# A macaron block on one core: the router's logit difference on VectorE, the three-part split of B without casts, and nine steps of the slot table moved by one or two slots

## The reference, cut to what matters

```python
x = x + 0.5 * ffn(layernorm(x))        # f = 0
x = x + mamba(layernorm(x))
x = x + 0.5 * ffn(layernorm(x))        # f = 1

def ffn(x):                            # 8 experts of width 176, top 2; shared part of width 352
    logits, idx = top_k(x @ Wg, 2)
    w = one_hot(idx) weighted with softmax(logits)
    y = sum_e w[:, e] * ((silu(x @ W1[e]) * (x @ W2[e])) @ W3[e])
    return y + (silu(x @ Ws1) * (x @ Ws2)) @ Ws3

def mamba(x):                          # inner width 256, 16 states
    x_in, z = split(x @ W_in + b_in)
    xc = silu(conv4(x_in)); B, C = split(xc @ W_xp + b_xp); delta = softplus(xc @ W_dt + b_dt)
    h = exp(delta * A) * h + delta * xc * B         # scan over 256 tokens, for each of 16 states
    y = (sum over states of h * C + D * xc) * silu(z)
    return alpha * normalised(x + y @ W_out + b_out) + beta
```

## Time and profile before

| | |
|---|---|
| median of 3 runs | 1952.55 us (1949.0 to 1955.74) |
| the profiled execution | 1954.8 us, its span 1953.0 us |
| PE busy | 1685.0 us, 86% |
| DVE busy | 1528.1 us, 78% |
| POOL busy | 1435.9 us, 74% |
| ACT busy | 1216.9 us, 62% |
| mean granted TensorE clock | 0.950 of full speed |

### The profile page before, as it was taken

One profiled execution on the slowest core, in us unless ns is written; L12 is line 12 of the kernel. 1 busy time (PEld: TensorE's weight loads), 2 busy tenths in 40 slices (PEclk: granted clock), 3 DMA queues, 4 the chain that ended last, 5 costly groups with the idle time before them and its releaser, 6 DMA issues.

```text
span 1953.0 us, 27826 instructions
## 1 busy us (share of the span) xinstructions
PE 1685.0 (86%) x7378; PEld 1006.3 (52%) x7378; DVE 1528.1 (78%) x2337; ACT 1216.9 (62%) x1828; POOL 1435.9 (74%) x1350
## 2 busy tenths in 40 slices
PE   2896868999989899899989899898989999967488
PEld 1553535555545555555545555555555555544255
DVE  2237988988878888788878898888889898888732
ACT  1265657676856767586766767676676767665322
POOL 2336767788878778688877878788877878887853
PEclk9897969999989999999999999999999999988698
DMA  4124756776766857577665767667585867767742
GB/s 133 38 82 117 186 119 175 166 184 164 177 159 152 192 146 190 142 169 183 166 167 145 186 166 174 170 158 189 147 197 138 204 165 173 180 149 176 160 102 65
DMA packets 121342, 305.10 MB, mean 156 GB/s; under 512 B 19299, under 2 KB 40518, under 8 KB 106822
## 3 DMA queue, kind: packets, MB, share of 16 engines
q0 software_dynamic: 18432, 125.84, 31.9%
q1 hardware_dynamic: 94976, 173.07, 30.7%
q10 hardware_dynamic: 7750, 4.10, 0.8%
HBM read 167.67 MB, written 5.24 MB: 89 GB/s over the span
## 4 chain that ended last, share of the span: by engine, by line
PE 37%; issue 18%; POOL 14%; DVE 13%; DMA 11%; ACT 5%; ACTq 1%; DVEq 1%; POOLq 0%; SPq 0%
PE ps_y L1062 9%; DVE hist L903 6%; POOL prod L579 5%; POOL gated L517 5%; DMA yacc<-prod 5%; PE ps_h1b L1048 5%; PE ps_h2b L1070 5%; PE ps_h1a L1048 4%; PE ps_h2a L1070 4%; PE ps_m L1019 3%; DMA wrow<-w_rows 3%; PE ps_m L1113 3%; DMA out<-xres 2%; PE ps_m L1009 2%; DVE gated L883 1%
## 5 line engine op out<-in xcount | busy, mean ns | idle before, releaser
L579 POOL TENSOR_TENSOR prod<-hist,crow 128x1024 f32<-128x1024 f32 x224 | 566.6, 2530 | 239.6 <-DVE hist L903 237.7
L1062 PEld LDWEIGHTS ps_y<-down_w,gated 128*128 128x128 f32 (+1 forms) x3584 | 474.3, 196 | 267.4 <-issue 165.0
L903 DVE TENSOR_TENSOR_SCAN hist<-decay,ps_db 128x1024 f32<-128x1024 f32 x256 | 583.6, 2280 | 2.9
L517 POOL TENSOR_TENSOR gated<-gated,silu 128x512 f32<-128x512 f32 x352 | 484.6, 1440 | 93.9 <-DVE gated L883 81.2
L1062 PE MATMUL ps_y<-down_w,gated 128*128 128x128 f32 (+1 forms) x3584 | 489.5, 281 | 40.8 <-DVE xres L890 22.7
L855 DVE TENSOR_TENSOR ps_db<-du,ps_db 128x1024 f32<-128x1024 f32 x256 | 313.1, 1223 | 185.4 <-PE ps_db L1030 183.0
L667 ACT ACTIVATE decay<-delta,a_neg 128x510 f32<-128x510 f32 x512 | 327.0, 709 | 3.6 <-DVE hist L903 2.2
L687 ACT ACTIVATE silu<-ps_h1a 128x512 f32<-128x512 f32 (+1 forms) x224 | 133.0, 594 | 223.5 <-PE ps_h1a L1048 223.3
L1070 PE MATMUL ps_h2a<-xnT,up_w 128*128 128x512 f32 (+1 forms) x448 | 236.2, 609 | 22.9 <-DVE gated L883 22.7
L1048 PE MATMUL ps_h1b<-xnT,up_w 128*128 128x512 f32 x448 | 240.7, 619 | 3.5 <-ACT silu L687 3.5
L1070 PE MATMUL ps_h2b<-xnT,up_w 128*128 128x512 f32 x448 | 231.5, 599 | 8.5 <-DVE gated L883 8.5
(11 more groups left out here) (139 smaller groups left out, 1915.3 us busy)
## 6 DMA issues: line engine op xcount, KB each, us to landing
yacc<-prod POOLq DMA_DIRECT2D x112, 1024.0 KB, 9.4
crow<-c_rows SPq DMA_DIRECT2D x128, 512.0 KB, 4.6
wrow<-w_rows SPq DMA_DIRECT2D x320, 128.0 KB, 5.0
wrow<-w_rows SPq DMA_DIRECT2D x64, 224.0 KB, 7.2
wrow<-w_rows SPq DMA_DIRECT2D x64, 192.0 KB, 6.2
...
```

Of the source, the lines that this page charges most:

```text
L517: nc.gpsimd.tensor_tensor(gated[:, pos % NGATE, :], gated[:, pos % NGATE, :], silu[:, (pos + NCHUNK * f_parity(of, f)) % NSILU, :], ALU.mu ...
L579: nc.gpsimd.tensor_tensor(prod[:, (pair - 1 + odd) % 2, s % 2, :, :], hist[:, s % 2, :, :], c_all, ALU.mult).then_inc(prod_done, 1)
L903: nc.vector.tensor_tensor_scan(hist[:, s % 2, :, :].rearrange("p h t -> p (h t)"), decay[:, s % NA, :, :, :].rearrange("p h b t -> p (h b ...
L1062: ins = nc.tensor.matmul(ps_y[:, t * C:(t + 1) * C], gated[0:rd, posd % NGATE, t * P:(t + 1) * P], down_w[0:rd, jd, :], start=(posd == 0 a ...
```

## The change

1. `drop0` and `drop1` leave POOL. DVE makes the difference inside `route`, where a one-element memset stood between the maxima and the indices.
2. `bparts` is done without casts: the first part comes straight from PSUM plus bias with a bf16 output, the others are subtractions with bf16 outputs. Six instructions and four waits become five and a memset, with three waits.
3. Table: `addy0` one slot earlier (4 to 3); `route0` one later (10 to 11), `tilt0` one earlier (13 to 12); `stats1` and `scale1` one earlier (to 19 and 20); `route1`, `tilt1`, `weights1` one earlier (to 25, 27, 28); `delta` two later (24 to 26).
4. The last chunk of the second layer moves from slot 16 to 17, and with it the work that follows it by one, two and four slots.
5. SP issues the rows of C (`c6`) ahead of the weights' rows `w0:3`.

```diff
-        0: ["stats0"], 1: ["scale0"], 2: ["norm0"], 3: ["fold"], 4: ["addy0", "xT0"], 5: ["stats2", "scale2", "logits0"],
+        0: ["stats0"], 1: ["scale0"], 2: ["norm0"], 3: ["addy0", "fold"], 4: ["xT0"], 5: ["stats2", "scale2", "logits0"],
...
-    UNIT = {s: (1, pos) for pos, s in enumerate((0, 1, 2, 3, 4, 5, 6, 7, 8, 10, 12, 14, 15, 16))}
+    UNIT = {s: (1, pos) for pos, s in enumerate((0, 1, 2, 3, 4, 5, 6, 7, 8, 10, 12, 14, 15, 17))}
...
-                        elif step == "drop0" and enters(k) or step == "drop1" and tail(k):
-                            pool.wait_ge(top_ready, route_no(k, step) + 1)
-                            nc.gpsimd.tensor_tensor(drop[:], top[:, :, 0], top[:, :, 1], ALU.subtract
-                                                    ).then_inc(drop_ready, 1)
...
                             dve.wait_ge(top_ready, route_no(k, step) + 1)
-                            nc.vector.memset(carrier[:], 0.0)
+                            nc.vector.tensor_tensor(drop[:], top[:, :, 0], top[:, :, 1], ALU.subtract
+                                                    ).then_inc(drop_ready, 1)
...
-                            nc.vector.tensor_tensor(
-                                bc[:], ps_m[:, 0:TILES * 2 * NS].rearrange("p (t n) -> p t n", t=TILES),
-                                b_xp_b[:].unsqueeze(1).to_broadcast([P, TILES, 2 * NS]), ALU.add
-                            ).then_inc(misc_taken, 1)
-                            dve.wait_ge(misc_taken, turn(k, "xproj"))
-                            chain = Chain(dve, dve_bc, 4, k + 1)
-                            split(chain, bc[:, :, 0:NS], brem[:], brem2[:], bparts, NS).then_inc(bparts_ready, 1)
+                            chain = Chain(dve, dve_bc, 3, k + 1)
+                            rows_in = ps_m[:, 0:TILES * 2 * NS].rearrange("p (t n) -> p t n", t=TILES)
+                            bias = b_xp_b[:].unsqueeze(1).to_broadcast([P, TILES, 2 * NS])
+                            hi, md, lo = (bparts[:, :, 32 * q:32 * q + NS] for q in range(PARTS))
+                            nc.vector.tensor_tensor(bc[:], rows_in, bias, ALU.add)
+                            chain.link(nc.vector.tensor_tensor(hi, rows_in[:, :, 0:NS], bias[:, :, 0:NS], ALU.add))
+                            nc.vector.tensor_tensor(brem[:], bc[:, :, 0:NS], hi, ALU.subtract).then_inc(misc_taken, 1)
+                            chain.link(nc.vector.tensor_tensor(md, bc[:, :, 0:NS], hi, ALU.subtract))
+                            chain.link(nc.vector.tensor_tensor(lo, brem[:], md, ALU.subtract))
+                            nc.vector.memset(carrier[:], 0.0).then_inc(bparts_ready, 1)
```

More of the change, by code:

```diff
@@ L837, in stats_no @@
                 return before(k, stats_list) + stats_list(k).index(which)
-            def split(chain, whole, rem, rem2, parts, width):
-                hi, md, lo = (parts[:, :, 32 * q:32 * q + width] for q in range(PARTS))
-                chain.link(nc.vector.tensor_copy(hi, whole))
-                chain.link(nc.vector.tensor_tensor(rem, whole, hi, ALU.subtract))
-                chain.link(nc.vector.tensor_copy(md, rem))
-                chain.link(nc.vector.tensor_tensor(rem2, rem, md, ALU.subtract))
-                return nc.vector.tensor_copy(lo, rem2)
             def input_term(g, par, s):
```

1 line of the change is left out of this document (removed), and 12 rows, old and new, of tables (PLAN, SP_PLAN).

## The result

Before: 1954.14 us, median of 4 runs (1949.0 to 1957.9). Changed: 1922.26 us, median of 4 runs (1919.37 to 1923.06). The ratio is 0.9836, interval 0.981 to 0.9862: faster by 31.9 us, 1.6%. The profiled execution took 1919.37 us with a span of 1917.5; PE is busy 1670.5 us (87%), DVE 1546.6 (81%), POOL 1433.3 (75%), ACT 1222.6 (64%).

What follows compares the result with a forecast made beforehand. PE was taken as the bound, through its idle waits. The terms summed to 4.3 us per body, rounded to 4.0, times 12 is 48, plus 7 outside: 1954.8 - 55 = 1900, or 1898 at the median; range 1880 to 1918.

Steps and rivals of the forecast that it cites:

- the rival at 1935: New waits, at `dt1` for ACT and at `row_b` for state 14, take most of the gain; 1935 us, chance 0.18.
- `addy0`, +1.7: `addy0` one slot sooner: PE's wait of 1.74 us for `xres` goes, gaining 1.7 us per body.
- `resid`, +0.3: `resid` ahead of the routing: PE's 0.65 us wait for `rtok` goes, half counted, +0.3 us per body.
- The last chunk, -0.7: Last chunk in slot 17: the 0.81 us wait for `bounce` is covered, a 1.5 wait for `dpre` comes; -0.7 per body.
- `stats1`, 0: `stats1` one slot sooner moves into DVE's wait of 2.43 us in slot 19; no gain or loss.
- The split, +0.3: Split without casts: the wait for POOL moves to the subtraction, two small instructions behind it are saved; +0.3 us per body.
- `route1` ahead of the scan, -0.7: Routing with `drop` on DVE before scan 13: the scan comes 2.3 us later, PE's `row_b` waits 1.4; -0.7 per body.
- `weights1`, +2.4: `weights1` one slot sooner, no `drop` on POOL: PE's whole 2.49 us wait for `wtok` goes; +2.4 per body.
- The clock, +0.8: Slow PE matmuls behind the wait for `wtok` go in six of twelve bodies; +0.8 us per body on average.
- The rest, +0.2: Rows of weights that DVE waits for in slot 26 of some bodies, now later in its order; +0.2 us per body.
- The four bodies outside, 7 us: The four bodies outside the loop, with the same waits, were to give some 7 us.
- The slower rival: DVE's routing waits twice for POOL, at `drop` and at `hot`, delaying every scan behind; 1976 us, chance 0.09.

Runs made afterwards that it cites:

- The early release: Changed kernel with the PSUM tile given back by a memset right behind its two reads instead of by `brem`; 1916.96 us, ratio 0.9797.
- The routing put back: Changed kernel with `route1`, `tilt1`, `weights1` and `delta` in their old slots, `drop` still on DVE; 1934.7 us, ratio 0.9895.
- the second run: The changed kernel measured again, unedited, on the chip of the other kernels of its call; 1920.86 us, ratio 0.9823.
- the parts measured alone: Kernel before with only `addy0` in slot 3 (1935.88 us), only the new split (1949.29), or only the last chunk, `stats1`, `scale1` and `c6` moved (1960.57).
- the first group: First of three groups of kernel runs, each beside the kernel before on its own chip; there eleven counted runs of before spread from 1941.75 to 1967.34 us.

## Why the prediction was right, and where its numbers were not

The direction held, and the mechanism in the main: PE's waits went, and DVE's slack at the end of the body paid for them (2.80 to 4.46 before, 1.3 to 2.2 after). The forecast was 56 us and 31.9 came; 1922 lies above the forecast's own range (1880 to 1918), inside that of 8 in 10, and nearer to the rival at 1935 than to 1898. The body was to be 107 us and is 108.5. By its own steps:

- **`addy0`, +1.7: right.** Alone it shortens the loop by 14.6 us, and the time by 13 to 34, where 12 times 1.7 is 20.
- **`resid`, +0.3: not measured alone.** The waits of PE for `rtok`, 7.8 us over the twelve bodies, are gone.
- **The last chunk, -0.7, and `stats1`, 0: about right together.** The wait for `dpre` was to be 1.5 and is 0.52. I had not seen that POOL's `gated`, one slot later with its chunk, would be late by 0.70. 0.8 gained less 1.2 lost is -0.4; the measurement says 0 with 0.5 per body either way (6 us over twelve). In the changed kernel the transpose waits 0.36 for `zs` too, which the step had as a bound, and 0.8 less 1.6 is close to the -0.7. `stats1` waits 2.26 for POOL's `xres` (835.11), about the 2.43 that DVE waited there before.
- **The split, +0.3: right in what happens, too small to be measured.** `brem` takes 2.16 at the median, the write of the first part 0.21. The Trainium skill ("SBUF — State Buffer", Who interferes with whom) says that a DVE instruction with two inputs in SBUF contends with a GpSimd instruction that reads SBUF, and the trace agrees for 0.21 against 2.16. What I missed is that `brem` also gives the PSUM tile back, so that PE waits 1.40 for it. The early release shows that this wait costs nearly nothing, since other waits for DVE take its place.
- **`route1` ahead of the scan, -0.7: right at DVE, not on POOL.** `drop` takes 1.35 against the 1.4 expected, `hot` 0.69 against 0.5. (The items of the sum, 0.35, 1.4, 0.9 and 0.5, give 3.15 and not 3.4.) PE's wait for the scan is 0.41 in every second body against 1.4. The step that failed is that I followed the later scan to `row_b` alone. POOL's product of state 13 waits for that scan as well (2.86 us in each body, where before it was 0 to 2.2), and a `gated` that PE needs stands behind it.
- **`weights1`, +2.4, "The whole wait goes": this is where the forecast missed.** The wait for `wtok` did go, as said. But PE meets 2.34 for POOL's `gated` in the slot before, because of the later product. The routing put back exchanges one for the other (29.9 us of waits for `wtok` against 27.9 for `gated`), and moving that one `gated` ahead of the product gives about 15 us more (1922.26 and 1920.86 against 1906.37). That is most of the 24 us that were missing.
- **The clock, +0.8: half of it, and for the same reason.** What the clock lacks falls from 0.17 to 0.12 of a body, which is 0.05 times 110 us or 0.5 per body (0.3 by the second run, with 0.14). Behind the new wait PE's clock still falls in six bodies of twelve. In body 7 the four groups behind it take from 976.39 to 981.01, 4.62 us, where body 6 takes 2.94 for the same four (869.09 to 872.03): 1.7 lost in such a body, 0.8 on average over twelve, which I had booked as won. With the `gated` earlier the clock is at 1.00 (the level of 2.4 GHz) in all twelve bodies, and PE is busy 100.8 per body instead of 101.4. The step also priced a fall of the clock at 1.7 wherever it stands. Ahead of the back edge it cost more, as told below.
- **The rest, +0.2: right in direction.** DVE's waits for rows of weights fall from 8.6 us in seven bodies to 0.3 in one.
- **The four bodies outside, 7 us:** the span outside the loop was 617.8 and is 615.2, so 2.6 came.
- **The slower rival** (routing that waits twice for POOL) did not form: `drop` at most 2.15 and `hot` at most 0.71, never both long. The rival in which new waits take most of the gain came nearest in kind, with 1935; it named ACT and `row_b`, and the wait stood on POOL. The sign of being wrong, `tilt0` held for more than 1 us right behind `drop`, did not show: it waits 0.5.

What no step of the sum had is the back edge of the loop. DVE at the end of body 7 before, PE behind it, and DVE at the same place in the changed kernel:

```profile
1014.03 0.69 DVE L883 TENSOR_TENSOR gated<-ps_h2b,wrow 128x512 f32<-128x512 f32 x1 [5.15 <-issue]
```

```profile
1014.78 1.12 PE L1070 MATMUL ps_h2b<-xnT,up_w 128*128 128x512 f32 x2 [2.21 <-DVE gated L883]
```

```profile
989.77 0.69 DVE L869 TENSOR_TENSOR gated<-ps_h2b,wrow 128x512 f32<-128x512 f32 x1 [2.31 <-PE ps_y L1052]
```

Between its last `input_term` and its first `gated` behind the jump DVE stands for 5.2 to 5.8 us at three of the five back edges before, for nothing that the profile shows, and PE then waits 2.2 to 3.4 for that `gated`. At the other two DVE stands 2.5 and 2.9. In the five kernels that keep the wait for `wtok`, 12 of 25 back edges are long (5.0 to 6.9). In all twelve PE's products behind that wait ran slowly (1.2 to 1.9 us for a pair in place of 1.02), so that the last `input_term` had waited 4.3 to 4.5; in none of the other thirteen did they, and it had waited 2.8. In the nine kernels without the wait for `wtok`, DVE stands 2.1 to 3.2 at all 45. So before, a fall of the clock ahead of the back edge went with a body 3.6 us longer (115.3 against 111.7 on average), where I had booked 1.7; in the changed kernel it goes with 1.5 (110.7 against 109.2). About 2 us at each of three back edges, 6 of the loop's 33, therefore came without a term in the sum, and as far as the forecast goes they are luck. Why a late DVE stands longer at the jump is open.

PE behind the new wait in body 7 of the changed kernel, for the step on the clock:

```profile
976.39 1.26 PE L1052 MATMUL ps_y<-down_w,gated 128*128 128x128 f32 x8 [2.35 <-POOL gated L516]
977.45 1.92 PE L1060 MATMUL ps_h2b<-xnT,up_w 128*128 128x512 f32 x2
...
981.01 1.05 PE L1052 MATMUL ps_y<-down_w,gated 128*128 128x128 f32 x8
```

By their ratios the parts measured alone bring 23.5, 3.3 and -0.6 us. Of the 34.6 of the second run 8.4 are left for the routing, `resid` and `drop`, against 36 (12 times the sum of 0.3, -0.7, 2.4, 0.8 and 0.2) that I had given them. The routing put back costs 13.8 by the spans; the intervals of the first group are wide enough to hold both.

Open: what PE waits for at the loop's back edge where DVE is not late. In the changed kernel it stands there 1.4 to 2.4 us in each of five bodies, for nothing that the profile shows, where before had 0.8 and 1.3 in two and the waits for DVE's late `gated` in three; in all it is 9.6 us against 13.6. In the kernels with fewer other waits it grows again, to 13.1 and up to 18.6, so part of what they save is paid there. I have no experiment on it.
